# A recommender tower: VectorE turns the samples in 32x32 blocks, and the top layers run in two batches

## The chip, the cores and the metric

The kernel runs on one core of a Trainium2 chip. Its time is the device time of one launch in microseconds (us). Engines are named as in the profile: PE (TensorE matmuls, PEld for the loads of weights), DVE (VectorE), ACT (ScalarE), POOL (GpSimd) and SP (SyncE, which here only issues DMAs). PSUM is the memory of eight banks that matmuls write to, SBUF the memory that all engines share.

## The reference, cut to what matters

For 512 samples, 32 embedding rows of 32 numbers each are gathered from 32 tables. Two layers of a compressed interaction network follow, then three dense layers.

```python
e = stack([tbl_f[ids[:, f]] for f in range(32)], axis=1)      # 512 x 32 fields x 32 dims
x0 = prev = e
for W in (filter_0, filter_1):                                # (32*32 -> 128), (32*128 -> 128)
    z = einsum('bhd,bmd->bhmd', x0, prev).reshape(b, h * m, d)
    prev = relu(einsum('bpd,pn->bnd', z, W[0]))
    outs.append(prev)
z = sum(concatenate(outs, axis=1), axis=-1)                   # 512 x 256
h = concatenate([z, dense_ctx], axis=1)                       # 512 x 272
h = maximum(h @ W_top1 + b_top1, 0)                           # 512 x 512
h = maximum(h @ W_top2 + b_top2, 0)                           # 512 x 256
y = h @ W_top3                                                # 512 x 1
```

Everything is float32. The kernel splits the operands of the large products into a high and a low part and multiplies three pairs of them in the faster fp32r format.

## The kernel before, in words

The 512 samples are four blocks of 128, and the 32 dims are eight groups of 4. A chunk is one block and one group: 128 samples times 4 dims, thus 512 columns. There are 32 chunks. Two chunks make one turn of the loop (UNROLL), and the first and the last turn are written out.

In a chunk PE walks through 32 slots of three matmuls of 512 columns each (line 870): layer 2 of the chunk, into four banks that DVE reads and two that ACT reads. DVE multiplies each 128 columns by a field's number and adds them up (line 762, eight such MACs for four slots); ACT multiplies the other half (line 561) and POOL sums these with accumulating DMAs and adds (lines 358, 365, 372). Between the slots stands the work for the next chunks, each at a slot that a constant gives (lines 51 to 67): DVE multiplies pairs of fields for chunk c + 1 (DVE_PAIR, slots 0, 4, 8 and 12 of chunk c, line 622), ACT and POOL split them (lines 496 and 381), and PE multiplies them with layer 1's filters into cur_bank (PE_PRODUCT, slots 17 to 24, line 808); the product of slot 22 needs DVE's line 626, which stands ahead of DVE's MACs of slot 20.

The pairs need the fields of the samples with the samples along the columns, and shifted copies of them. That is done two chunks ahead, for chunk c + 2 during chunk c. At slot 0 ACT copies the 32 x 4 numbers of each of the 128 samples to turn_in (line 474). At slot 4, after DVE has read the sums out of the same bank (line 641), PE transposes this 128x128 block into cur_bank (line 787). At slot 5 ACT copies it to turned (line 479). SP writes turned to a scratch buffer in DRAM in two DMAs of 512 B rows, the 32 fields and 16 of them once more (line 312), waits for both, and loads it back in six DMAs, once as it is (x4) and five times shifted (shifts, line 320). ACT copies x4 to its PSUM bank at slot 29, and DVE's first pair reads the shifts at slot 0 of chunk c + 1. Every engine runs its own instructions in order; they wait for each other with semaphores alone. A register counts the chunks in the loop.

The start does chunk 0's layer 1 without DRAM: DVE copies the gathered fields in spread order (line 712), PE transposes them (line 839), and DVE multiplies. Chunk 1 already goes through DRAM (the calls with c = 1).

At the end DVE and POOL sum what is left of the last block of 128 samples (lines 769 to 781). PE has by then started top 1: it needs z1 (layer 1's sums), the dense inputs and z2 (layer 2's). z1 and the dense part are multiplied for all 512 samples (lines 901 and 902), z2 for the first 384 (line 905), and then PE waits for the last 128. These are transposed (line 816), copied by ACT (line 592) and multiplied (line 911). Relus on ACT (line 596), top 2 (line 917), relus (line 600), top 3 (line 922), a copy (line 603) and one DMA of the 512 results follow, each over all 512 samples. Float32 matmuls take two instructions each in the profile.

## Time and profile before

| | |
|---|---|
| time, median of 3 runs | 891.64 us (889.85 to 893.33) |
| the profiled execution's own time | 892.28 us |
| its span, first to last instruction | 890.5 us |
| PE busy | 837.7 us, 94% |
| DVE busy | 763.7 us, 86% |
| ACT busy | 727.2 us, 82% |
| POOL busy | 663.0 us, 74% |
| mean granted clock of PE | 0.996 of 2.4 GHz |
| mean traffic of the DMA engines | 140 GB/s |

A busy share is one over the whole span. Matmuls overlap, so a busy PE says less than the distance from one matmul's start to the next one's. In the rows below, what stands in brackets is the idle time of that engine ahead of the instruction and what ended it.

### The profile page before, as it was taken

To read this page: it belongs to the slowest core of one execution; us is meant where nothing else is said; L and a number is where in the kernel's file an instruction comes from. 1 tells how busy PE (TensorE), PEld (TensorE's weight loads), DVE (VectorE), ACT (ScalarE), POOL (GpSimd) and SP (SyncE) were. 2 spreads that over 40 slices of the span, in tenths; PEclk is the share of its full clock that TensorE was granted. 3 is DMA by queue.
4 is the path that set the end of the run, shared out by engine and by line. 5 is a ranking of instruction groups with operands and counts; after the bars stand their busy time and mean duration, and the time that the engine had idled before them with its cause. 6 is when DMAs were issued, how large, how long until landed. Compare 5 with 4: busy or idle time off the path is not lost.

```text
span 890.5 us, 18079 instructions
## 1 busy us (share of the span) xinstructions
PE 837.7 (94%) x3607; PEld 669.2 (75%) x3607; DVE 763.7 (86%) x2394; ACT 727.2 (82%) x2418; POOL 663.0 (74%) x645
## 2 busy tenths in 40 slices
PE   0179999999999999999999999999999999999997
PEld 0158888888888788888888878888888888888873
DVE  4148989999988899999999999999999999999993
ACT  2257889998888899888888889888888989888872
POOL 7776898878787888878888888866666676666651
PEclk9999999999999999999999999999999999999999
DMA  7035776667667666667567656676577656665450
GB/s 195 13 91 123 173 167 147 147 128 156 152 149 165 161 155 148 132 146 160 145 158 173 157 139 136 140 166 144 146 169 169 150 144 128 138 159 145 79 95 0
DMA packets 59773, 124.40 MB, mean 140 GB/s; under 512 B 9377, under 2 KB 18145, under 8 KB 59746
## 3 DMA queue, kind: packets, MB, share of 16 engines
q0 software_dynamic: 22240, 68.17, 40.8%
q1 hardware_dynamic: 37506, 55.96, 19.7%
q14 instruction: 21, 0.17, 0.1%
q8 instruction: 6, 0.10, 0.0%
HBM read 54.99 MB, written 3.05 MB: 65 GB/s over the span
## 4 chain that ended last, share of the span: by engine, by line
PE 79%; POOL 9%; issue 4%; DVE 4%; DMA 2%; ACT 0%; SPq 0%; DVEq 0%; POOLq 0%; ACTq 0%
PE bank L870 67%; PE bank L808 10%; POOL rows L346 4%; DVE acc L762 2%; POOL pair_low L381 2%; POOL rows_next L396 1%; POOL parts L358 1%; PE bank L917 1%; POOL w_sb L365 1%; DMA parts<-parts 1%; PE bank L876 1%; DMA shifts<-x_scratch 1%; PE bank L787 0%; POOL half L365 0%; DVE acc L772 0%
## 5 line engine op out<-in xcount | busy, mean ns | idle before, releaser
L561 ACT ACTIVATE parts<-bank,x 128x128 f32<-128x128 f32 x2048 | 590.2, 380 | 99.0 <-PE bank L870 88.5
L762 DVE SCALAR_TENSOR_TENSOR acc<-bank,x,acc 128x128 f32<-128x128 f32 x1792 | 484.7, 341 | 45.0 <-PE bank L870 44.9
L870 PE MATMUL bank<-w_high,cur_high 128*128 128x512 f32 x1024 | 403.8, 394 | 3.2 <-DVE acc L762 2.4
L870 PE MATMUL bank<-w_low,cur_high 128*128 128x512 f32 x1024 | 399.9, 391 | 0.0
L870 PE MATMUL bank<-w_high,cur_low 128*128 128x512 f32 x992 | 388.6, 392 | 0.0
L870 PEld LDWEIGHTS bank<-w_high,cur_high 128*128 128x128 f32 x1024 | 192.6, 188 | 46.0 <-DVE acc L762 3.4
L870 PEld LDWEIGHTS bank<-w_low,cur_high 128*128 128x128 f32 x1024 | 192.7, 188 | 40.4
L870 PEld LDWEIGHTS bank<-w_high,cur_low 128*128 128x128 f32 x992 | 186.5, 188 | 40.6
L381 POOL TENSOR_TENSOR pair_low<-pair,pair_high 128x512 fp32r<-128x512 f32 x124 | 158.7, 1300 | 27.9 <-ACT pair_high L496 25.5
L365 POOL TENSOR_TENSOR half<-parts 128x512 f32<-128x512 f32 x64 | 82.8, 1294 | 93.0 <-DMA parts<-parts 92.9
L396 POOL DMA_INDIRECT rows_next<-table_dram,ids_next x96 | 98.0, 1021 | 30.6 <-issue 30.3
L358 POOL DMA_DIRECT2D parts<-parts x126 | 114.5, 1070 | 4.4 <-issue 4.3
L622 DVE TENSOR_TENSOR pair<-bank,shifts 128x512 f32<-128x512 f32 x124 | 84.2, 679 | 4.9 <-DMA shifts<-x_scratch 4.9
L365 POOL TENSOR_TENSOR w_sb<-parts 128x512 f32<-128x512 f32 x62 | 80.1, 1313 | 3.1 <-DMA parts<-parts 3.0
L496 ACT CAST pair_high<-pair 128x512 fp32r<-128x512 f32 x124 | 79.8, 644 | 2.0 <-DVE pair L622 2.0
L762 DVE SCALAR_TENSOR_TENSOR acc<-bank,x,parts 128x128 f32<-128x128 f32 x128 | 41.7, 346 | 16.0 <-PE bank L870 12.6
L808 PE MATMUL bank<-pair_high,w_low 128*128 128x512 f32 x124 | 49.2, 397 | 0.0
L808 PE MATMUL bank<-pair_high,w_high 128*128 128x512 f32 x124 | 48.9, 394 | 0.2
L808 PE MATMUL bank<-pair_low,w_high 128*128 128x512 f32 x124 | 49.0, 395 | 0.0
L822 PE MATMUL bank<-w_high 128*128 128x512 f32 x16 | 5.7, 531 | 40.9 <-DMA rows<-table_dram,ids_sb 40.9
L372 POOL TENSOR_TENSOR w_sb<-half 128x512 f32<-128x512 f32 x32 | 41.4, 1294 | 3.5
L346 POOL DMA_INDIRECT rows<-table_dram,ids_sb x32 | 34.4, 1074 | 12.1 <-issue 9.4
(92 smaller groups left out, 551.9 us busy)
## 6 DMA issues: line engine op xcount, KB each, us to landing
parts<-parts POOLq DMA_DIRECT2D x126, 512.0 KB, 6.1
shifts<-x_scratch SPq DMA_DIRECT2D x155, 256.0 KB, 3.9
x<-x_scratch SPq DMA_DIRECT2D x31, 256.0 KB, 2.9
x_scratch<-turned SPq DMA_DIRECT2D x31, 64.0 KB, 4.0
rows_next<-table_dram,ids_next POOLq DMA_INDIRECT x96
wt<-w_top_dram SPq DMA_DIRECT2D x2, 512.0 KB, 8.9
x_scratch<-turned SPq DMA_DIRECT2D x31, 32.0 KB, 3.9
rows<-table_dram,ids_sb POOLq DMA_INDIRECT x32, 2.4
```

The costliest lines, as they stand in the source:

```text
L346: nc.gpsimd.indirect_dma_start(out=rows[:, 0, f, :], out_offset=None, in_=tables[f], in_offset=bass.IndirectOffsetOnAxis(ids_sb[:, 0, f:f ...
L358: nc.gpsimd.dma_start(parts[q][ab][:, 0:width], parts[q][ab][:, width:2 * width], accum_op=ALU.add).then_inc(added[ab], 16)
L365: nc.gpsimd.tensor_tensor(half[t // 2 % 2][:, t % 2, :], src[:, 0:512], src[:, 512:1024], ALU.add).then_inc(tree, 1)
L372: nc.gpsimd.tensor_tensor(left[:, t % DC:t % DC + 2, :, :].rearrange("p t l n -> p t (l n)"), half[t // 2 % 2][:, :, 0:256], half[t // 2 % ...
L381: nc.gpsimd.tensor_tensor(pair_low[step - 1][:], pair[step - 1], pair_high[step][:].bitcast(FP32), ALU.subtract).then_inc(pair_low_done, 1)
L396: nc.gpsimd.indirect_dma_start(out=rows_next[:, f, :], out_offset=None, in_=tables[f], in_offset=bass.IndirectOffsetOnAxis(ids_next[:, f:f ...
L496: nc.scalar.copy(pair_high[step][:], pair[step - 1]).then_inc(pair_high_done, 1)
L561: ins = nc.scalar.activation(parts[q][ab][:, at:at + N2], act_bank[ab][:, i * N2:(i + 1) * N2], ACT.Copy, scale=x0[u][:, h, 2 * q + ab:2 * ...
L622: nc.vector.tensor_tensor(dst[:], fields, shifted, ALU.mult).then_inc(paired, 1)
L762: nc.vector.scalar_tensor_tensor(out=dst, in0=dve_bank[e % 2 * 2 + ab][:, i * N2:(i + 1) * N2], scalar=x0[u][:, h, 2 * q + ab:2 * q + ab + ...
L808: ins = nc.tensor.matmul(cur_bank[:], filters, products, start=step == order[0] and i == 0, stop=step == order[-1] and i == len(terms) - 1)
L870: return nc.tensor.matmul(dst[:], cur_half[u][:, cols], w1_half[:, fields], **flags)
```

## The change

The transposition for the way through DRAM moves from PE to DVE, whose transposition turns each 32x32 block by itself. turn_in and turned now hold the 16 repeated fields too (192 columns), which ACT copies at slot 0 with a second, smaller copy. DVE transposes at slot 8, ahead of that slot's pair. Which block goes where is left to the DMAs: SP writes four of them, one for each 32 partitions, in runs of 32 numbers. PE's transposition, ACT's copy out of PSUM and their semaphore go.

The top layers run for samples 0 to 383 and for the last 128 in turn, each with PSUM banks of its own. PE multiplies everything of the 384 that is known, the known part of the last 128, and half of top 2 of the 384 ahead of the transposition of the last z2; then the other half, and the rest of the last 128 behind it. ACT's relus and copies are split alike. SP waits for two copies of results and sends one DMA as before.

```diff
-ACT_TURN, PE_TURN, ACT_TURNED = 0, 4, 5
+ACT_TURN, DVE_TURN = 0, 8
+QUAD = 32
...
-        turn_in = sb("turn_in", [P, DC * F])
-        turned = sb("turned", [P, P])
+        turn_in = sb("turn_in", [P, DC * (F + SHIFTS)])
+        turned = sb("turned", [P, DC * (F + SHIFTS)])
...
-        a1_bank, a2_bank, y_bank = [bank[4], bank[5], bank[7], dve_bank[0]], dve_bank[1:3], dve_bank[3]
+        a1_bank, last_a1_bank = [x4_bank] + act_bank + [dve_bank[0]], dve_bank[1:4] + [cur_bank]
+        a2_bank, last_a2_bank = [x4_bank, act_bank[0]], [dve_bank[0], act_bank[0]]
+        last_z2_bank = act_bank[1]
+        y_bank, last_y_bank = x4_bank, act_bank[1]
...
-        WRITES, LOADS = 2, STEPS
+        WRITES, LOADS = P // QUAD, STEPS
...
                 sp.wait_ge(turned_ready, c)
                 to = x0_dram[u]
-                for first_field, fields in ((0, F), (F, SHIFTS)):
-                    if first_field > 0:
-                        wait(sp, paired, (c - 1) * STEPS)
-                    sp.dma_start(to[first_field:first_field + fields, :].rearrange("f (d b) -> (f d) b", d=DC),
-                                 turned[0:fields * DC, :]).then_inc(written, 16)
+                for b in range(0, P, QUAD):
+                    dst = bass.AP(to.tensor, to.offset + b, [[P, QUAD], [QUAD * P, (F + SHIFTS) * DC // QUAD], [1, QUAD]])
+                    sp.dma_start(dst, turned[b:b + QUAD, :].rearrange("i (k j) -> i k j", j=QUAD)).then_inc(written, 16)
                 sp.wait_ge(written, c * (WRITES * 16))
...
         def act_turn(act, c):
-            nc.scalar.copy(turn_in[:].rearrange("p (f d) -> p f d", d=DC), rows_of(c)).then_inc(turn_ready, 1)
-
-        def act_turned(act, c):
-            act.wait_ge(transposed, c)
-            wait(act, written, (c - 1) * (WRITES * 16))
-            nc.scalar.copy(turned[:], turn_bank[:, 0:P]).then_inc(turned_ready, 1)
+            fields = turn_in[:].rearrange("p (f d) -> p f d", d=DC)
+            nc.scalar.copy(fields[:, 0:F, :], rows_of(c)).then_inc(turn_ready, 1)
+            nc.scalar.copy(fields[:, F:, :], rows_of(c)[:, 0:SHIFTS, :]).then_inc(turn_ready, 1)
...
+        def dve_turn(dve, c):
+
+            dve.wait_ge(turn_ready, 2 * c)
+            wait(dve, written, (c - 1) * (WRITES * 16))
+            nc.vector.transpose(turned[:], turn_in[:]).then_inc(turned_ready, 1)
...
             first_copy(F - LAST_TABLES, F - LAST_TABLES, F)
+            dve_turn(dve, 1)
             dve.wait_ge(first_fields_ready, 3)
...
+                            if slot == DVE_TURN and not last:
+                                dve_turn(dve, c + 2)
                             if slot == DVE_SUM:
...
-        def pe_turn(pe, c):
-            pe.wait_ge(turn_ready, c)
-            wait(pe, summed, c - 1)
-            nc.tensor.transpose(turn_bank[:, 0:P], turn_in[:], ident[:]).then_inc(transposed, 1)
...
             if step == order[0]:
                 wait(pe, summed, c)
-                if turn:
-                    pe.wait_ge(turned_ready, c + 1)
...
             for i in range(H1 // P):
-                n = slice(i * P, (i + 1) * P)
                 if a1_bank[i] is x4_bank:
                     pe.wait_ge(folded, CHUNKS - 1)
+                elif a1_bank[i] is act_bank[0]:
+                    pe.wait_ge(act_prod, PAIRS * (2 * EACH))
                 if i == H1 // P - 1:
                     pe.wait_ge(mac, PAIRS * (2 * MACS) - 2 * HG)
-                nc.tensor.matmul(a1_bank[i][:], wt1[:, 0, n], z1[:], start=True, stop=False)
-                nc.tensor.matmul(a1_bank[i][:], wt1_dense[:, n], dense_sb[:], start=False, stop=False)
+                top1_known(a1_bank[i][:, three], i, three)
             pe.wait_ge(z2_ready, 1)
             for i in range(H1 // P):
-                nc.tensor.matmul(a1_bank[i][:, 0:B - P], wt1[:, 1, i * P:(i + 1) * P], z2[:, 0:B - P], start=False,
-                                 stop=False)
-            pe_z2(pe, BLOCKS - 1, BLOCKS)
+                nc.tensor.matmul(a1_bank[i][:, three], wt1[:, 1, i * P:(i + 1) * P], z2[:, three], start=False,
+                                 stop=True).then_inc(top_product, 1)
+            pe.wait_ge(mac, PAIRS * (2 * MACS))
+            for i in range(H1 // P):
+                top1_known(last_a1_bank[i][:, 0:P], i, last)
+            top2(a2_bank[0][:, three], 0, three, 0)
+            pe.wait_ge(z2_step, 4)
+            nc.tensor.transpose(last_z2_bank[:, 0:P], z2_rows[:, BLOCKS - 1, :], ident[:]).then_inc(z2_turned, 1)
+            top2(a2_bank[1][:, three], 1, three, 0)
             pe.wait_ge(z2_ready, 2)
             for i in range(H1 // P):
-                n = slice(i * P, (i + 1) * P)
-                nc.tensor.matmul(a1_bank[i][:, B - P:], wt1[:, 1, n], z2[:, B - P:], start=False,
+                nc.tensor.matmul(last_a1_bank[i][:, 0:P], wt1[:, 1, i * P:(i + 1) * P], z2[:, last], start=False,
                                  stop=True).then_inc(top_product, 1)
...
+            top3(y_bank[0:1, three], three, H1 // P)
+            top2(last_a2_bank[0][:, 0:P], 0, last, THREE_PRODUCTS)
+            top2(last_a2_bank[1][:, 0:P], 1, last, THREE_PRODUCTS)
+            top3(last_y_bank[0:1, 0:P], last, THREE_PRODUCTS + H1 // P)
```

top1_known multiplies z1 and the dense part, top2 and top3 run the four and the two products of a group of outputs, each behind the relus that it needs; three and last are the columns 0 to 383 and 384 to 511. ACT takes, in order: the four relus of the 384, the copy of the last z2, the two relus of top 2 of the 384, the four relus of the last 128, the copy of the 384 results, the two relus of the last 128, and their copy.

## Rows read from the trace of the kernel before

**Rows 1.** The page's chain that ended last, shares of the span by engine.

```profile
PE 79%; POOL 9%; issue 4%; DVE 4%; DMA 2%; ACT 0%; SPq 0%; DVEq 0%; POOLq 0%; ACTq 0%
```

**Rows 2.** PE: timelines around two transpositions (start, us, what), a chain piece, a wait.

```profile
392.36 0.39 PE L870 MATMUL bank<-w_high,cur_low 128*128 128x512 f32 x1
392.93 0.39 PE L870 MATMUL bank<-w_low,cur_high 128*128 128x512 f32 x1
...
417.45 0.39 PE L870 MATMUL bank<-w_high,cur_low 128*128 128x512 f32 x1
418.22 0.40 PE L870 MATMUL bank<-w_low,cur_high 128*128 128x512 f32 x1
...
843.48 4.55 PE bank L870 x20
...
PEld bank L787 <- issue: 4.2, 13, 0.4
```

**Rows 3.** Timelines of DVE and PE over a chunk; one group by lines.

```profile
406.31 0.69 DVE L626 TENSOR_TENSOR pair_hl<-bank,pair_hl 64x512 fp32r<-64x512 f32 x1
407.14 0.41 PE L808 MATMUL bank<-pair_hl,w_half_hl 128*128 128x512 f32 x1
...
422.88 0.68 DVE L622 TENSOR_TENSOR pair<-bank,shifts 128x512 f32<-128x512 f32 x1
423.47 2.15 DVE L762 SCALAR_TENSOR_TENSOR acc<-bank,x,acc 128x128 f32<-128x128 f32 x8
429.27 0.74 DVE L762 SCALAR_TENSOR_TENSOR acc<-bank,x,parts 128x128 f32<-128x128 f32 x2 [0.39 <-PE bank L870]
...
L762 DVE SCALAR_TENSOR_TENSOR acc<-bank,x,parts 128x128 f32<-128x128 f32 x128 | 41.7, 346 | 16.0 <-PE bank L870 12.6 <-ACT parts L561 2.1
```

**Rows 4.** Groups by line: a DVE operation on 384 words.

```profile
L651 DVE TENSOR_TENSOR rows_next<-w_sb 128x384 f32<-128x384 f32 x1 | 0.6, 558 | 0.0
```

**Rows 5.** DMA queues and landings (page), and timelines of SP and DVE.

```profile
q0 software_dynamic: 22240, 68.17, 40.8%
q1 hardware_dynamic: 37506, 55.96, 19.7%
...
shifts<-x_scratch SPq DMA_DIRECT2D x155, 256.0 KB, 3.9
...
420.90 1.65 SPq L312 DMA_DIRECT2D x_scratch<-turned  x2
425.95 3.13 SPq L320 DMA_DIRECT2D shifts<-x_scratch  x5
...
442.58 0.68 DVE L622 TENSOR_TENSOR pair<-bank,shifts 128x512 f32<-128x512 f32 x1
```

**Rows 6.** Timeline of the start, and a window (PE, PEld, DVE, ACT, POOL busy; PEclk, DMA).

```profile
49.05 1.09 PE L839 MATMUL bank<-ident,parts 128*128 128x128 f32 x8 [2.41 <-DVE parts L712]
51.56 0.92 SPq L312 DMA_DIRECT2D x_scratch<-turned  x2
62.63 0.69 DVE L622 TENSOR_TENSOR pair<-bank,shifts 128x512 f32<-128x512 f32 x1 [4.94 <-DMA shifts<-x_scratch]
65.45 0.79 PE L870 MATMUL bank<-w_high,cur_high 128*128 128x512 f32 x1 [2.41 <-DVE acc L762]
...
65.40:68.70 3.30, 3.25 (x8) 2.58 (x9) 3.26 (x10) 1.62 (x7) 2.90 (x4) 0.50 0.19 45
```

**Rows 7.** PE's timeline of the end, and a window of it (columns as above).

```profile
865.84 1.10 PE L901 MATMUL bank<-x,wt 128*128 128x512 f32 x2 [0.65 <-ACT parts L561]
870.27 2.74 PE L905 MATMUL bank<-pair,wt 128*128 128x384 f32 x8
875.61 0.33 PE L816 MATMUL bank<-ident,rows_next 128*128 128x128 f32 x1 [2.59 <-DVE rows_next L780]
876.29 1.16 PE L911 MATMUL bank<-pair,wt 128*128 128x128 f32 x8 [0.35 <-ACT pair L592]
886.38 1.88 PE L922 MATMUL bank<-w_sb,wt 128*1 128x512 f32 x4
...
877.60:881.30 3.70, 3.68 (x5) 1.64 (x6) 0.00 (x0) 1.70 (x3) 0.00 (x0) 0.54 0.00 0
```

More of the change, by code:

```diff
@@ L29 @@
 BLOCKS = B // P
+THREE = B - P
 DC = 4
@@ L206, in dlrm_tower @@
         turn_ready = sem("turn_ready")
-        transposed = sem("transposed")
         turned_ready = sem("turned_ready")
@@ L578, in body @@
                                     act_x4(act, c + 2, u)
-                                if slot == ACT_TURNED and not last:
-                                    act_turned(act, c + 2)
                                 if slot == ACT_Z2 and last and u == UNROLL - 1:
                                     act.wait_ge(z2_turned, 1)
-                                    nc.scalar.copy(z2[:, 0:B - P], turn_bank[:, 0:B - P]).then_inc(z2_ready, 1)
+                                    nc.scalar.copy(z2[:, 0:B - P], z2_bank[:, 0:B - P]).then_inc(z2_ready, 1)
             body_loop(act, body)
@@ L881, in body @@
                                 if slot in PE_PRODUCT and not (last and u == UNROLL - 1):
-                                    pe_product(pe, c + 1, PE_PRODUCT[slot], turn=not last)
-                                if slot == PE_TURN and not last:
-                                    pe_turn(pe, c + 2)
+                                    pe_product(pe, c + 1, PE_PRODUCT[slot])
                                 if slot == PE_Z2 and last and u == UNROLL - 1:
@@ L893, in _, with top1_known, top2 @@
             pe.wait_ge(z1_step, 2)
-            pe.wait_ge(act_prod, PAIRS * (2 * EACH))
+            three, last = slice(0, THREE), slice(THREE, B)
+            def top1_known(dst, i, columns):
+                n = slice(i * P, (i + 1) * P)
+                nc.tensor.matmul(dst, wt1[:, 0, n], z1[:, columns], start=True, stop=False)
+                nc.tensor.matmul(dst, wt1_dense[:, n], dense_sb[:, columns], start=False, stop=False)
+            def top2(dst, m, columns, relus_before):
+                for i in range(H1 // P):
+                    pe.wait_ge(top_relu, relus_before + i + 1)
+                    ins = nc.tensor.matmul(dst, wt2[:, i, m * P:(m + 1) * P], a1[:, i, columns], start=i == 0,
+                                           stop=i == H1 // P - 1)
+                ins.then_inc(top_product, 1)
@@ L895, in _, with top3 @@
+            def top3(dst, columns, relus_before):
+                for i in range(H2 // P):
+                    pe.wait_ge(top_relu, relus_before + i + 1)
+                    ins = nc.tensor.matmul(dst, wt3[:, i:i + 1], a2[:, i, columns], start=i == 0,
+                                           stop=i == H2 // P - 1)
+                ins.then_inc(top_product, 1)
             for i in range(H1 // P):
-                n = slice(i * P, (i + 1) * P)
                 if a1_bank[i] is x4_bank:
                     pe.wait_ge(folded, CHUNKS - 1)
+                elif a1_bank[i] is act_bank[0]:
+                    pe.wait_ge(act_prod, PAIRS * (2 * EACH))
@@ L920, in _ @@
-            for k in range(H2 // P):
-                pe.wait_ge(top_relu, H1 // P + k + 1)
-                ins = nc.tensor.matmul(y_bank[0:1, :], wt3[:, k:k + 1], a2[:, k, :], start=k == 0,
-                                       stop=k == H2 // P - 1)
-            ins.then_inc(top_product, 1)
+            top3(y_bank[0:1, three], three, H1 // P)
+            top2(last_a2_bank[0][:, 0:P], 0, last, THREE_PRODUCTS)
+            top2(last_a2_bank[1][:, 0:P], 1, last, THREE_PRODUCTS)
+            top3(last_y_bank[0:1, 0:P], last, THREE_PRODUCTS + H1 // P)
```

45 lines of the change are left out of this document (24 added, 21 removed).

## The prediction

> **What bounds the kernel now.** I read the page's chain that ended last first: PE has 79% of the span [rows 1]. Nearly all of that is the chunk loop, so the next question is how tight PE runs there and what else runs as tight. The timeline of PE shows matmuls that start every 0.2275 us (4.55 us for 20 [rows 2]); a chunk has 109 of them (32 slots of 3, and 13 for the next chunk's products), 24.8 us. So PE sets the pace, and time is won in the loop only where a matmul start is late. One such place is the transposition, at slot 4.
>
> The second view is VectorE's timeline over one chunk, because DVE is busy 86% of the span and PE's banks come free by its MACs. DVE runs without a pause from the MACs of slot 20 of one chunk to those of slot 12 of the next; only ahead of slot 16 does it wait for PE, 0.39 us in the chunk shown, and 12.6 us in all such waits, 0.41 us in each of 31 chunks [rows 3]. Ahead of slot 20 it waits another 1.4 us, but that is no spare time: DVE's low half of pair 16 (L626) ends at 407.00, PE's product that needs it starts at 407.14, and the MACs of slot 20 need the matmuls right behind that product [rows 3]. So PE and DVE form a ring through L626, the product of slot 22, slot 23 and the MACs of slot 20, and DVE's spare time per turn of the ring is the 0.41 us, and some 0.08 us of the 0.14 between L626 and the product: 0.49 us beside a PE that still has its transposition.
>
> The third view is the timeline of the end. PE is idle from 873.0 (870.27 + 2.74) to 875.61, when DVE's last sums reach it, and only then runs the last quarter of top 1, all of top 2 and top 3 in a row until 888.26; the granted clock was 0.54 from 877.6 to 881.3 (1.2 GHz for most of it), behind that idle time [rows 7].
>
> **The loop: what PE gives back.** In one chunk of two kinds the transposition costs PE 392.93 - 392.36 = 0.57 us for two matmul steps that take 0.455 without it, so 0.115; in the other kind 418.22 - 417.45 = 0.77, so 0.315, since it waits there for DVE's sum (L641) too; 13 of the 30 in the loop are of that kind [rows 2]. Together 13 x 0.315 + 17 x 0.115 = 6.1 us, 0.20 us a chunk. That is all that leaving it out can give: 6.1 us, if nothing takes its place. The wait for the sum goes too; pe_product keeps its own wait for summed, but 13 slots later.
>
> **The loop: what DVE takes on.** One transposition of 128x192 words a chunk, 30 times, ahead of the pair of slot 8, thus in the part without a pause. No row shows such an operation. A 128x512 pair takes 0.68 us and the next operation starts 0.59 after it (422.88 to 423.47 [rows 3]), so 0.09 of a duration is overlapped; a 128x384 add takes 0.56 [rows 4], so a word costs about 0.95 ns and 192 words some 0.37 us, which is 0.29 of DVE's time. Ends: nothing at all (0, if it ran inside gaps), and 0.59, what a 512-word operation takes. I take 0.30, next to the 384-word row. With PE 0.20 faster the ring leaves DVE 0.49 - 0.20 = 0.29 us: just used up. Two parties with no slack do not meet exactly in both kinds of chunk, so I take 0.04 a chunk off: the period falls by 0.16 us, 30 x 0.16 = 4.8 us. At 0.59 it would rise by 0.59 - 0.49 = 0.10, 3 us lost.
>
> The Trainium skill, "VectorE: DVE Perf Modes", section "The three transpose paths", has 390 ns on TensorE and 311 ns on VectorE for 128x128 in bf16, and says that VectorE turns 32x32 blocks only. By 311 x 1.5 = 0.47 us (an estimate from that page; no run here shows it), 0.38 of DVE's time, the loop would give 2.1 us (30 x 0.07) instead of 4.8; and its 390 ns is not what leaving out the PE transposition is worth here, since rows 2 show 0.12 to 0.32.
>
> **ACT, SP and the DMA queue.** ACT loses the PSUM copy of slot 5 and gets a 128x64 copy at slot 0, both about 0.3 us; it waits for PE again within the same chunk, so nothing. SP issues four writes in place of two, at 0.4 to 0.5 us each (0.92 for two [rows 6]), and its wait for paired goes, which DVE's order implies. The transposed rows are ready at about 423.3 in place of 420.9; the five shift loads were issued until 429.08 and land in 3.9; the next chunk's first pair reads them at 442.58 [rows 5]. So 442.6 - 433.0 = 9.6 us spare, less 2.4 for the later start and 0.9 for two more issues: 6.3 us are left for slower writes. The writes turn from 192 packets of 512 B into 768 of 128 B, 48 on each of 16 engines in place of 12. SP's queue spent 19.7% x 16 x 890.5 / 37506 = 75 ns on a packet [rows 5]: 36 more are 2.7 us, inside the 6.3. Costed at nothing. Later loads meet the accumulating DMAs longer; POOL, which waits for those, has its results used some chunk later.
>
> **The start.** The transposition of chunk 1 now stands on DVE ahead of the copies that PE's first transposes wait for (49.05), so that chain starts about 0.9 us later (the wait for ACT's two copies, and 0.37). But PE stood still for 2.41 us at 65.45 anyway, because DVE waited 4.94 us for chunk 1's shifts; the clock was 0.50 behind it [rows 6]. What counts is when the shifts land. The writes can be issued from about 49.6 in place of 51.56, the last of four at 51.0 in place of 52.0, so 1 us earlier; 36 packets more on each engine take from nothing to 2.7 us. Between 1 us won and 1.7 lost I take 0; should the stall shrink enough to keep the clock, 1.6 us more come back (eight matmuls at 0.43 for 0.23).
>
> **The end.** Work on 384 columns costs three quarters of that on 512. The order of PE after the loop, from rows 7:
> - known products of the 384: PE now starts with the bank that is free at once (x4_bank), so up to 0.65 us earlier (its wait for ACT at 865.84); four took (870.27 - 865.84) = 4.43, now 3.3: 865.2 to 868.5; z2's products 2.74: 871.3;
> - known products of the last 128: four at a quarter of 4.43 and some overhead, 1.5: 872.8;
> - top 2, first half of the outputs, 384 columns, 8 instructions as those of L905: 2.74: 875.55. ACT's relus run beside it. All that fills the idle time.
> - DVE's last sums come at 875.6 as before: transposition 0.33, 875.95; second half of top 2, 2.74: 878.7, which hides ACT's copy of z2; last quarter of top 1, 1.16: 879.85; top 3 of the 384, three quarters of 1.88: 881.25;
> - top 2 of the last 128, twice 1.16: 883.55; its last relu, 0.35 (as the gap ahead of 876.29): 883.9; top 3's last two instructions 0.3: 884.2 in place of 888.26.
>
> That is 4.1 us, and the copy of 128 results in place of 512 perhaps 0.1: 4.2. Of it, about 1.8 is the clock, which I expect to stay at 2.4 GHz since PE is no longer idle ahead of it. The lower end is 2.2 (the clock at half for as long as before), the upper 5.
>
> **Sum.** 4.8 + 0 + 4.2 = 9.0 us. The profiled execution took 892.28 (span 890.5 and 1.8 around it), so 883.3; it lies 0.64 above the median of 891.64, so I forecast 882.6. Best ends: 6.1 + 2.6 + 5 = 13.7, 878; worst of the plain terms: loop -3, end 2.2, start -1.7: 894.
>
> **Rivals.**
> 1. *DVE becomes the bound.* The transposition takes 0.45 to 0.59 of its time (blocks filled and drained, an operation that overlaps less). For: a pause of 0.41 us a chunk is all that DVE has. Against: it is shorter than any of the 512-word operations. Loop from 0.0 to -3, end 4.2: 887.4 to 890.5.
> 2. *The end keeps its half clock, or ACT's chain of small relus stretches it.* For: the clock fell once there, and the last stretch has short matmuls. Against: no PE idle time over 0.4 us in the new order. End 2.2 in place of 4.2: 884.6.
> 3. *Slower: the writes come too late.* Place: SP's wait for the four writes, and behind it six loads; it decides once the writes take over 6.3 us longer. At what a packet cost on POOL's queue (40.8% x 16 x 890.5 / 22240 = 261 ns [rows 5]) 36 more packets are 9.4 us: 3.1 us a chunk, 93 us over 30, about 975. Against: SP's own queue shows 75 ns. In the Trainium skill, "DMA: Bandwidth & Descriptors", the table "Specifications" asks for 512 B or more for line rate and has a read-modify-write below that; this rule speaks against the change, 512 to 128 B, and no run here shows what such writes to DRAM cost.
> 4. *The split does nothing*, since top 2's second half stands ahead of the last quarter of top 1: the end gives 1, 885.8. Against: that half hides ACT's copy and would have to run anyway.
>
> **How the numbers follow.** Forecast 0.57, rival 1 0.17, rival 2 0.16, rival 3 0.06, rival 4 0.04. Half a per cent, about what a measurement tells from no change, is 4.5 us: faster is below 887.2, slower above 896.1. Forecast, rivals 2 and 4 fall under faster (0.77) and the lucky end of rival 1 adds 0.03; the rest of rival 1 and a hundredth of rival 3 give same, 0.15; the rest of rival 3 slower, 0.05. The range runs from the best ends, 878, to the far end of rival 1, 890, and leaves out rival 3 and what overruns the ends.
>
> **What would show it.** No L787 on PE, and 0.2275 us between all starts around slot 4; the transposition at about 0.37 us on DVE with a following start 0.3 later; DVE's wait ahead of slot 16 gone, a chunk period of 25.0 us in place of 25.16; no wait of DVE or ACT for shifts or x4 beyond the first chunk; PE without idle time over 0.5 us behind the loop, clock 1.0, and its end 4 us earlier in relation to the last MAC. Wrong: a chunk period at or above 25.16, waits of L626's product that grow, shifts that land after the next chunk begins, or a clock of 0.5 in the end.

## The result, and the profile after

The changed kernel takes 886.12 us (median of 6 runs, 882.99 to 888.07) against 890.50 us for the kernel before on the same chip (6 runs); the ratio is 0.9947, with a 95% interval from 0.9932 to 0.9962. The time lies inside the range and the sign was right, but 4.4 us came where 9.0 were forecast. The profiled execution took 882.99 us, span 881.2; it is the fastest of the six, so a second profile of the same kernel (changed_again, below, 886.55 us) stands beside it wherever the two differ.

The first thing to read is where the time of a span lies. The cuts are the starts of the first matmul with cur_low in chunk 1 and in chunk 31 (line 876 before, 885 after):

| us | before | after | changed_again |
|---|---|---|---|
| start and chunk 0 | 86.61 | 84.92 | 84.74 |
| chunks 1 to 30 | 756.48 | 753.72 | 756.15 |
| chunk 31 and the end | 47.41 | 42.56 | 43.81 |
| span | 890.5 | 881.2 | 884.7 |

So in the execution nearer to the median the loop won little, and of the 4.85 us that chunk 31 and the end won in the other, 3.6 were left; where those 1.25 us lie is shown behind the end's profile.

The chain that ended last still belongs to PE (it answers to [rows 1]):

```profile
PE 80%; POOL 9%; issue 5%; DVE 3%; DMA 2%; ACT 0%; POOLq 0%; DVEq 0%; ACTq 0%
```

PE around slot 4 of the same chunk as in [rows 2] (start, duration, what): the starts are 0.23 us apart, and no transposition stands between them.

```profile
388.86 0.39 PE L879 MATMUL bank<-w_low,cur_high 128*128 128x512 f32 x1
389.09 0.39 PE L879 MATMUL bank<-w_high,cur_low 128*128 128x512 f32 x1
389.32 0.39 PE L879 MATMUL bank<-w_high,cur_high 128*128 128x512 f32 x1
```

DVE, against [rows 3, 4]: the transposition with the operation behind it, the MACs of slot 16 and the low half of pair 16 in the next chunk's timeline; then the transposition's line (duration in ns, least/median/greatest), and the group of MACs that waited at slot 16.

```profile
394.23 0.36 DVE L637 STREAM_TRANSPOSE turned<-turn_in 128x192 f32<-128x192 f32 x1
394.52 0.65 DVE L631 TENSOR_TENSOR pair<-bank,shifts 128x512 f32<-128x512 f32 x1
...
426.55 0.74 DVE L780 SCALAR_TENSOR_TENSOR acc<-bank,x,parts 128x128 f32<-128x128 f32 x2
428.87 0.70 DVE L641 TENSOR_TENSOR pair_hl<-bank,pair_hl 64x512 fp32r<-64x512 f32 x1
...
L637 DVE STREAM_TRANSPOSE turned<-turn_in x31: 358/366/379, 49.6 to 796.4; 128x192 f32<-128x192 f32 x31
...
L780 DVE SCALAR_TENSOR_TENSOR acc<-bank,x,parts 128x128 f32<-128x128 f32 x128 | 41.8, 346 | 6.5 <-ACT parts L560 3.3 <-PE bank L879 1.2
```

The next operation starts 0.29 us after the transposition, and the pause ahead of slot 16 is gone: 6.5 us in that group in place of 16.0, of it 1.2 for PE in place of 12.6. A chunk that nothing disturbs now takes 25.04 us in place of 25.17 (medians of the odd and of the even chunks, averaged).

SP's queue and the landings of the page, and SP's issues for chunk 16's way through DRAM, answer to [rows 5]:

```profile
q1 hardware_dynamic: 56354, 55.96, 21.0%
...
parts<-parts POOLq DMA_DIRECT2D x126, 512.0 KB, 6.7
shifts<-x_scratch SPq DMA_DIRECT2D x155, 256.0 KB, 3.9
...
420.73 1.81 SPq L316 DMA_DIRECT2D x_scratch<-turned  x4
424.41 3.11 SPq L323 DMA_DIRECT2D shifts<-x_scratch  x5
```

The shifts land as fast as before. The accumulating DMAs (parts<-parts) land later, after 6.7 us where the page of before has 6.1, and POOL waits longer for them. Its largest waits in the kernel before (us in total, times, longest):

```profile
POOL half L365 <- DMA parts<-parts: 92.9, 58, 3.9
POOL mark L355 <- DVE parts L762: 27.3, 25, 2.0
```

The same two waits in the changed kernel:

```profile
POOL half L368 <- DMA parts<-parts: 119.9, 60, 5.9
POOL mark L358 <- DVE parts L780: 1.7, 6, 0.4
```

The 27.3 us for which POOL waited at the mark, the instruction ahead of the next accumulating DMA, were its spare time. After, that wait is 1.7 us. Where the spare time runs out shows in chunk 13, which took 25.11 us before and 25.85 after. Timelines of SP, POOL and PE there, in the kernel before:

```profile
374.94 0.53 SPq L320 DMA_DIRECT2D x<-x_scratch  x1
...
380.20 1.83 POOL L358 DMA_DIRECT2D parts<-parts  x2
385.58 1.29 POOL L365 TENSOR_TENSOR half<-parts 128x512 f32<-128x512 f32 x1 [3.55 <-DMA parts<-parts]
...
390.72 1.04 POOL L422 COPY rows<-rows_next 128x1024 f32 x1
403.43 2.55 POOL L381 TENSOR_TENSOR pair_low<-pair,pair_high 128x512 fp32r<-128x512 f32 x2
...
405.51 0.40 PE L870 MATMUL bank<-w_high,cur_low 128*128 128x512 f32 x1
405.75 0.39 PE L808 MATMUL bank<-pair_high,w_high 128*128 128x512 f32 x1
```

The same instructions of chunk 13 in the changed kernel:

```profile
373.42 0.53 SPq L323 DMA_DIRECT2D x<-x_scratch  x1
...
377.04 1.84 POOL L361 DMA_DIRECT2D parts<-parts  x2
383.75 1.29 POOL L368 TENSOR_TENSOR half<-parts 128x512 f32<-128x512 f32 x1 [4.87 <-DMA parts<-parts]
...
388.87 1.04 POOL L425 COPY rows<-rows_next 128x1024 f32 x1
401.57 2.53 POOL L384 TENSOR_TENSOR pair_low<-pair,pair_high 128x512 fp32r<-128x512 f32 x2
...
402.09 0.40 PE L879 MATMUL bank<-w_high,cur_low 128*128 128x512 f32 x1
402.90 0.50 PE L819 MATMUL bank<-pair_high,w_high 128*128 128x512 f32 x1 [0.42 <-POOL pair_low L384]
```

Read from top to bottom: the loads start 5.26 us ahead of the accumulating DMA before, and 3.62 after. The DMA lands in 5.38 and in 6.71 us. Behind it on POOL stand the sums, the copy of the next block's rows (only in chunks 5, 13 and 21, where a block of samples is changed), a copy of row numbers, the next accumulating DMA, two gathers of rows (from 392.78 to 395.17 after; they and the copy of row numbers are missing in chunk 21), and then the splits of the pairs. Before, the pair that the product needs is split at 404.7 (half of the two from 403.43), 1.05 us ahead of PE's product at 405.75; after, at 402.84, and the product's start is 0.81 us behind the matmul ahead of it where 0.23 is the pace. Chunk 21 is in time in every profile, though it has the copy too: without the gathers its split is ready 13.9 us behind the chunk's first matmul with cur_low in place of 16.3.

The start, against [rows 6]: the first pair, and the window where PE stood still before (busy time and instructions of PE, PEld, DVE, ACT, POOL; PEclk, DMA share, GB/s).

```profile
60.68 0.69 DVE L631 TENSOR_TENSOR pair<-bank,shifts 128x512 f32<-128x512 f32 x1 [0.28 <-DMA shifts<-x_scratch]
...
65.40:68.70 3.30, 3.30 (x16) 2.72 (x15) 3.30 (x13) 3.24 (x12) 2.90 (x4) 1.00 0.13 21
```

The wait for shifts is 0.28 in place of 4.94 us, and PE runs 16 matmuls in a window that had 8, at a granted clock of 1.00 in place of 0.50. But PE's first transposes now run at 0.50 (50.3 to 52.5), behind an idle time of 2.48 us; before, they ran at 1.00 behind 2.41. This is not the change's own: top_only and end_warm below, which keep the old start, have the half clock there too, and turn_only, which has the new one, has not.

The end, PE's timeline and a window over all of it, against [rows 7]:

```profile
860.62 0.81 PE L905 MATMUL bank<-x,wt 128*128 128x384 f32 x2
...
863.91 2.74 PE L932 MATMUL bank<-pair,wt 128*128 128x384 f32 x8
...
867.78 2.79 PE L911 MATMUL bank<-w_sb,wt 128*128 128x384 f32 x8
871.27 0.33 PE L939 MATMUL bank<-ident,rows_next 128*128 128x128 f32 x1 [0.70 <-DVE rows_next L798]
871.44 2.75 PE L911 MATMUL bank<-w_sb,wt 128*128 128x384 f32 x8
874.02 1.05 PE L943 MATMUL bank<-pair,wt 128*128 128x128 f32 x8
875.00 1.45 PE L918 MATMUL bank<-w_sb,wt 128*1 128x384 f32 x4
876.38 2.05 PE L911 MATMUL bank<-w_sb,wt 128*128 128x128 f32 x16
878.37 0.91 PE L918 MATMUL bank<-w_sb,wt 128*1 128x128 f32 x4
...
860.00:881.20 21.20, 18.42 (x85) 11.70 (x83) 11.00 (x17) 7.68 (x20) 5.14 (x6) 1.00 0.00 1
```

From the transposition of the last z2 to PE's last end it is 8.01 us (871.27 to 879.28); before it was 12.65 (875.61 to 888.26). The clock stays at 1.00, though PE still waits 0.70 us for the last z2.

This stretch takes 8.00 us in changed_again as well. What is longer there lies in chunk 31, where DVE's first sum for z1 and POOL's sum of parts run beside each other. The two in the profile of after, then in changed_again:

```profile
845.61 2.43 POOL L368 TENSOR_TENSOR w_sb<-parts 128x512 f32<-128x512 f32 x1 [2.90 <-DMA parts<-parts]
845.67 1.22 DVE L755 TENSOR_TENSOR w_sb<-sum 128x1024 f32<-128x1024 f32 x1
...
847.81 1.29 POOL L368 TENSOR_TENSOR w_sb<-parts 128x512 f32<-128x512 f32 x1 [2.90 <-DMA parts<-parts]
847.93 2.26 DVE L755 TENSOR_TENSOR w_sb<-sum 128x1024 f32<-128x1024 f32 x1
```

One of the two takes 1.0 to 1.1 us longer than the other time. Where POOL's record starts 0.06 us or less ahead of DVE's, POOL's is the long one; where it starts 0.09 us or more ahead, DVE's is, DVE's next MACs come later, and PE's last matmul of the chunk is 1.3 us late (0.8 in light_halves). This holds in all 14 profiles: the kernels with PE's transposition are all of the first kind, those with DVE's all of the second, except the profile of after. Why POOL comes some 0.05 us sooner there was not tested.

### The profile page after: what moved, and what is told of

It is laid out like the page before. It is cut to its first block, busy times and chain, and to the rows that moved or that the text cites. A ratio compares the mean times of both kernels' runs of the same rounds, so it can differ in the third digit from the quotient of the medians.

```text
span 881.2 us, 18094 instructions
## 1 busy us (share of the span) xinstructions
PE 832.6 (94%) x3608; PEld 669.4 (76%) x3608; DVE 771.7 (88%) x2425; ACT 724.7 (82%) x2425; POOL 662.0 (75%) x645
## 4 chain that ended last, share of the span: by engine, by line
PE 80%; POOL 9%; issue 5%; DVE 3%; DMA 2%; ACT 0%; POOLq 0%; DVEq 0%; ACTq 0%
PE bank L879 68%; PE bank L819 10%; POOL rows L349 4%; DVE acc L780 2%; POOL pair_low L384 2%; DMA parts<-parts 1%; POOL w_sb L368 1%; POOL rows_next L399 1%; PE bank L885 1%; POOL parts L361 1%; PE bank L911 1%; PE bank L850 1%; DVE acc L790 0%; POOL half L368 0%; DMA rows<-table_dram,ids_sb 0%
## 5 line engine op out<-in xcount | busy, mean ns | idle before, releaser
L879 PEld LDWEIGHTS bank<-w_high,cur_high 128*128 128x128 f32 x1024 | 192.3, 188 | 48.2 <-DVE acc L780 6.4
L375 POOL TENSOR_TENSOR w_sb<-half 128x512 f32<-128x512 f32 x32 | 41.4, 1294 | 3.6
```

The costliest lines, as they stand in the source:

```text
L375: nc.gpsimd.tensor_tensor(left[:, t % DC:t % DC + 2, :, :].rearrange("p t l n -> p t (l n)"), half[t // 2 % 2][:, :, 0:256], half[t // 2 % ...
L879: return nc.tensor.matmul(dst[:], cur_half[u][:, cols], w1_half[:, fields], **flags)
```

## The experiments

All are timed beside the kernel before. "Late" chunks are those over 0.3 us above the undisturbed period; 8, 9 and 18 are late in every kernel, by 1.8 us in sum in the profile of before, where it is always PE's product with pair_high and w_high that starts late (0.44 to 0.50 us behind the matmul ahead of it).

| kernel | median us (runs) | before | ratio [95%] | undisturbed period | late, us | chunk 31 and end |
|---|---|---|---|---|---|---|
| changed_again | 885.83 (6) | 890.41 | 0.9939 [0.9922, 0.9955] | 25.04 | 4.9 | 43.8 |
| turn_only | 890.29 (12) | 890.41 | 0.9996 [0.9984, 1.0009] | 25.03 | 5.1 | 48.3 |
| top_only | 885.53 (5) | 890.41 | 0.9935 [0.9922, 0.9949] | 25.18 | 2.2 | 42.5 |
| turn_slot4 | 887.55 (7) | 890.41 | 0.9968 [0.9949, 0.9988] | 25.10 | 5.0 | 43.8 |
| small_runs | 893.37 (9) | 890.79 | 1.0030 [1.0017, 1.0043] | 25.19 | 2.4 | 47.2 |
| late_before | 890.71 (12) | 890.79 | 1.0002 [0.9991, 1.0013] | 25.19 | 1.7 | 48.2 |
| top_turn6 | 883.36 (5) | 890.79 | 0.9911 [0.9898, 0.9924] | 25.07 | 3.0 | 42.5 |
| turn_twice | 890.02 (12) | 890.79 | 0.9989 [0.9980, 0.9999] | 25.19 | 4.5 | 43.8 |
| light_halves | 885.71 (5) | 891.10 | 0.9940 [0.9926, 0.9953] | 25.03 | 4.7 | 43.3 |
| light_before | 890.10 (11) | 891.10 | 0.9991 [0.9982, 1.0000] | 25.18 | 2.3 | 48.3 |
| end_warm | 889.32 (11) | 891.10 | 0.9981 [0.9972, 0.9990] | 25.18 | 3.2 | 45.8 |
| long_runs | 885.31 (5) | 890.65 | 0.9949 [0.9935, 0.9962] | 25.05 | 4.6 | 43.9 |

**The two parts alone.** First the changed kernel again, then each half of the change on the kernel before.

> The changed kernel as it is, for its spread. The six executions known so far run from 882.99 to 888.07 us, with the profiled one at the lowest; the forecast's sum holds in that one (9.3 us against 9.0), so the 3.5 us between it and the median are what is to be explained. Theory A (POOL falls behind: the shift loads now start 2.7 us later and meet the accumulating DMAs that POOL waits for, and in the profiled execution POOL's waits for those are already 119.9 us against 92.9): the median is 885 to 887 again, and this profile, if it is of a slower execution, shows more stretches in which the product of pairs waits for pair_low (3 in the first profile), each with a chunk period of 25.7 us or more; first and last chunk as in the first profile. Theory B (the start or the clock): the chunk periods are as in the first profile (mean 25.13 us over 29 chunks), and the difference lies ahead of chunk 1 or behind chunk 31.

turn_only has DVE's transposition and the four writes with the old top layers; top_only has the new top layers with PE's transposition:

```diff
 turn_only
-ACT_TURN, PE_TURN, ACT_TURNED = 0, 4, 5
+ACT_TURN, DVE_TURN = 0, 8
...
 top_only
-        a1_bank, a2_bank, y_bank = [bank[4], bank[5], bank[7], dve_bank[0]], dve_bank[1:3], dve_bank[3]
...
+        a2_bank, last_a2_bank = [x4_bank, act_bank[0]], [dve_bank[0], act_bank[0]]
...
```

> Only the transposition on DVE and its writes; the top layers as before the change. Theory A: the loop's gain of 2.8 us and the start's 2 are mostly lost in most executions, so 888 to 890 us, with the same spread of some 5 us. Theory B: 885 to 887 where the start goes well, and a spread that comes from the start. Forecast of the prediction for this part alone: 4.8 us won.

> Only the top layers in two batches; the transposition on PE as before. Both theories: the end gains 4.5 to 4.9 us as in the first profile of the changed kernel (47.4 us from the last chunk's start to the end against 42.6), so 885.6 to 886.2 us, and the spread is that of the kernel before (under 1.5 us in five of six executions). If the end's gain depends on how PE leaves the loop, it is under 3 us here.

In changed_again theory A holds for the loop: the median is 885.83 and PE waits four times for pair_low, 2.2 us in all. But 1.25 us of the difference between the two profiles lie in chunk 31, which neither theory named. top_only alone wins 4.9 us and turn_only 0.1, so the whole gain that can be measured is the end's. In turn_only the undisturbed period does fall by 0.13 us, 30 x 0.134 = 4.0 us, but chunks 5 and 13 are late by 0.8 and 1.9 us, and 8, 9 and 18 a little later than before: 5.1 - 1.8 = 3.3 us are given back. The rest went in chunk 31, which is 1.3 us longer there by DVE's long sum. From the transposition of the last z2 on, that profile is 0.4 us shorter (12.26 us against 12.65), so that chunk 31 and the end together have 48.3 us against 47.4; kernels with the old end take 12.3 to 13.5 us for that last stretch.

**When the way through DRAM starts.** The changed kernel with the transposition at slot 4:

```diff
-ACT_TURN, DVE_TURN = 0, 8
+ACT_TURN, DVE_TURN = 0, 4
```

> The changed kernel with DVE's transposition at slot 4 in place of 8: the writes and loads start 2.7 us earlier, about where they were before the change. Theory A: POOL's waits for the accumulating DMAs fall back towards 93 us, pair_low is late less often, and the median falls to 882 to 883.5 with a smaller spread. Theory B: no change against the changed kernel (885 to 887). A third possibility: PE waits at slot 13 for the MACs of slot 4, which now end 0.3 us later with 0.2 to spare; then the period grows by about 0.1 us and the median is 887 or more.

The median, 887.55 us, is that of the third possibility, though the period grew by 0.06 us only. The late chunks stay (5.0 us), because the loads did not start earlier: at slot 4 the four writes took 3.41 us to issue and SP's loads came 6.45 us behind the first of them (3.67 in the changed kernel, both in chunk 12).

Two experiments put one half each of what the change does to the way through DRAM into the kernel before: runs of 128 B in four writes at the old slot, and the old two writes four slots later.

```diff
 small_runs
-        WRITES, LOADS = 2, STEPS
+        WRITES, LOADS = 4, STEPS
...
+                    for half in range(2):
+                        n, at = fields * DC, half * F
+                        dst = bass.AP(to.tensor, to.offset + first_field * COLS + at, [[P, n], [2 * F, 2], [1, F]])
...
 late_before
-ACT_TURN, PE_TURN, ACT_TURNED = 0, 4, 5
+ACT_TURN, PE_TURN, ACT_TURNED = 0, 4, 9
```

> The kernel before, with PE's transposition, but the same bytes written in four DMAs of 128 B runs in place of two of 512 B runs (768 packets a chunk in place of 192). Theory A1 (the short runs hold up the accumulating DMAs that POOL waits for): POOL's waits for those rise from 93 to 110 us or more, its wait for DVE ahead of the next pair falls from 27 to under 8, parts lands in 6.5 us or more, more products wait for pair_low, and the time is 891 to 893. Theory A2 (the later start of writes and loads does it): POOL's waits stay under 97 us and the time is within 1 us of the kernel before.

> The kernel before, but ACT copies PE's transposed block out at slot 9 in place of 5, so that writes and loads start 1.5 to 2.7 us later; everything else, the 512 B runs too, as before. A1: POOL's waits for the accumulating DMAs stay under 97 us and the time is within 1 us of the kernel before. A2: they rise to 110 us or more and the time is 891 to 893. If both this and the short runs raise them by some 10 us, it is both.

Each takes part of POOL's spare time without a measurable stall in the loop: POOL waits 106.2 and 109.0 us for its DMAs (92.9 before), which land in 6.6 us, and its spare time at the mark falls to 14.5 and 10.9 us. By these waits it is both, as the expectation has it; A2's time for late_before, 891 to 893, did not come. small_runs loses 2.6 us, and its one profile puts most of them at the start, not in the loop: 86.90 us against 84.4 in late_before, both at a granted clock of 1.00, with chunk 1's loads 4.35 us behind its first write where the kernel before has 2.23. (The profile of before has 86.61 there for another reason: its clock fell to 0.50 behind DVE's wait for shifts.) Neither alone gives back in the loop what turn_only gives back.

**Is it that POOL has too much to do?** The changed kernel, and the kernel before, with POOL's last addition on half its columns:

```diff
-                nc.gpsimd.tensor_tensor(left[:, t % DC:t % DC + 2, :, :].rearrange("p t l n -> p t (l n)"),
-                                        half[t // 2 % 2][:, :, 0:256], half[t // 2 % 2][:, :, 256:512], ALU.add).then_inc(tree, 1)
+                nc.gpsimd.tensor_tensor(left[:, t % DC:t % DC + 1, :, :].rearrange("p t l n -> p t (l n)"),
+                                        half[t // 2 % 2][:, 0:1, 0:256], half[t // 2 % 2][:, 0:1, 256:512], ALU.add).then_inc(tree, 1)
```

> The changed kernel, but POOL's last add of each pair of tiles (sum_halves) covers half of its columns, so half of layer 2's sums on POOL are left out; POOL saves some 0.57 us twice a chunk and nothing else changes. Theory POOL (the loop's gain is lost because POOL has no slack left beside the slower accumulating DMAs): POOL's wait for DVE ahead of the next pair comes back to 20 us or more, the late chunks (5, 8, 9, 13, 18) shrink to under 2 us of excess in all, and the median falls from 885.8 to 882 to 883.5. Theory DVE and PE alone (the ring is the bound and POOL's waits are only its symptom): no change, 885 to 886.5.

> The same edit on the kernel before (half of POOL's last add left out). It has 27 us of slack on POOL already and three late chunks of 1.75 us in all. Theory POOL: 0 to 1.7 us faster, 889 to 890.7, so that the changed kernel with this edit leads it by 6.5 to 7.5 us in place of 4.6. If the lead stays 4.6, POOL is not where the loop's gain went.

My theory there was POOL's work, and its forecasts fell: the lead over light_before is 4.4 us, the late chunks stayed (4.7 us), and POOL spent the time that it was given in the same wait (us, times, longest, in light_halves):

```profile
POOL half L368 <- DMA parts<-parts: 140.7, 62, 6.5
```

In chunk 13 POOL issues the accumulating DMA 0.56 us earlier than in changed_again (10.07 us ahead of the chunk's first matmul with cur_low in place of 9.51), yet the first sum starts 2.04 us ahead of that matmul in place of 2.16: the landing did not follow the issue. The late chunks also have a second cause there. PE's wait for pair_low is only 0.06 us in that chunk (0.91 in changed_again), but PE then waits 0.52 us for DVE's low half of pair 16, since ACT waited 1.33 us for POOL's sum of parts and DVE 1.13 us for ACT. A late landing thus reaches PE in two ways, and the edit shortens the second by half as much as the first.

**Is it the short runs?** The changed kernel, with each write storing one run of 768 B for each partition:

```diff
-                    dst = bass.AP(to.tensor, to.offset + b, [[P, QUAD], [QUAD * P, (F + SHIFTS) * DC // QUAD], [1, QUAD]])
+                    dst = bass.AP(to.tensor, to.offset + b * (F + SHIFTS) * DC, [[(F + SHIFTS) * DC, QUAD], [1, (F + SHIFTS) * DC]])
```

> The changed kernel, but each of the four writes stores its 32 partitions in runs of 192 numbers (768 B) one behind another, as many bytes at the same slot; the scratch buffer then holds the numbers in another order, so the fields are mixed (the operands have other values, the work is the same). Theory A, the short runs of 128 B give the gain back: POOL's waits for its DMAs fall from 120 to some 108 us as in late_before, the median landing of its accumulating DMAs from 6.7 to 6.5 or less, the rows copies of chunks 5 and 13 are within 1.6 us of their chunk's first matmul, PE is not late in these two chunks, and the time falls by 1.5 to 3 us below the changed kernel's 886: 883 to 884.5. Theory B, it is the later writes and loads with the shorter period, whatever the runs: landing 6.6 or more, chunks 5 and 13 as late as before (0.6 to 1.9 us), 885.5 to 886.5. If only SP's issue of four writes counts, nothing moves either, and the start's wait for shifts stays near 0.3 us.

Theory B holds in the time, in the landing (6.7 us) and in chunk 5, which is late by 1.3 us; chunk 13 is in time. With a third fewer packets on SP's queue POOL waits as long. SP's queue on the page of long_runs, and POOL's wait:

```profile
q1 hardware_dynamic: 36514, 55.96, 20.0%
...
POOL half L368 <- DMA parts<-parts: 119.0, 61, 5.6
```

What goes with the lateness of chunks 5 and 13 is when the loads start. This table has chunks 5 and 13 of several kernels, from the timelines of SP, POOL and PE; the first two columns are measured from the chunk's first matmul with cur_low, and the last is the chunk's time above the undisturbed period.

| kernel, chunks 5 / 13 | loads start | rows copied | accumulating DMA issued to its second sum | late |
|---|---|---|---|---|
| before | -14.9 / -14.9 | 0.3 / 0.9 | 7.4 / 7.9 | 0 / 0 |
| late_before | -14.1 / -14.1 | 1.6 / 1.6 | 8.2 / 8.6 | 0 / 0 |
| small_runs | -13.8 / -14.5 | 1.8 / 0.9 | 7.6 / 7.9 | 0.2 / 0 |
| long_runs | -13.0 / -14.0 | 2.8 / 1.4 | 8.4 / 8.0 | 1.3 / 0 |
| after | -13.8 / -13.2 | 1.5 / 2.3 | 7.9 / 9.2 | 0 / 0.8 |
| changed_again | -13.1 / -13.1 | 2.4 / 2.9 | 8.0 / 9.8 | 0.9 / 1.4 |
| turn_only | -13.2 / -13.2 | 2.3 / 3.4 | 9.0 / 10.3 | 0.8 / 1.9 |
| turn_slot4 | -12.6 / -13.1 | 2.4 / 2.1 | 8.1 / 8.3 | 0.9 / 0.6 |
| light_halves | -13.3 / -13.2 | 2.7 / 2.5 | 10.7 / 10.5 | 1.2 / 1.0 |

In these two chunks, wherever the loads start at -13.8 or earlier the chunk is in time to 0.2 us; wherever they start at -13.3 or later, POOL's copy comes at 2.1 or later and the chunk is late. Even one kernel's two chunks part by this (after, long_runs). Without the copy and the gathers such a start does no harm: chunks 6, 10 and 14 of after have their loads at -13.0, -13.1 and -12.8 and are in time. With the copy alone, chunk 21 of turn_slot4 has its rows copied at 2.2 and is in time too.

That later transfers lengthen the accumulating DMA is what late_before shows: it moves only them and ACT's copy ahead of them, the loads by 0.8 us, and has 0.8 and 0.7 us more in the fourth column (in one profile; before, top_only and end_warm, whose loads start at -14.9, have 7.3 to 7.9). That this goes by way of the DMA engines is the reading that fits the trace's packets. From the DMA's issue to the second sum in chunk 13, SP's queue had packets under way for 1.57 us of the 16 engines' time before and for 2.86 after, 1.29 more, and the second sum came 1.30 us later (7.92 and 9.22); POOL's queue had 5.49 and 5.30 us. In the first 5 us the engines were busy throughout in both (DMA share 1.03 and 1.00). No run took the loads off these engines to prove it. In chunk 5 of changed_again only 0.6 of the 2.1 us come this way; the other 1.4 are the DMA's issue, at -8.3 in place of -9.7, since POOL, with its spare time at the mark gone, had not caught up from the late landing of half a chunk earlier.

**Is DVE's time used up?** The changed kernel with a second transposition, of 128 words, that nobody reads:

```diff
+            nc.vector.transpose(spare_turned[:], turn_in[:, 0:P])
```

> The changed kernel with a second transposition on DVE in each chunk, of 128x128 words into a buffer that nobody reads (some 0.22 us of DVE's time). Ring theory (DVE has no spare time left after the change): the period of undisturbed chunks rises from 25.03 to 25.2 or 25.25 us, 5 to 6.5 us in 30 chunks; POOL gets slack back, so up to 2.5 us of its late chunks go, and the time is 888.5 to 891. Theory that POOL alone sets the pace of the changed loop: under 1 us more, 885 to 887.

The spare transposition among the groups by line of turn_twice (busy us, mean ns of one, idle time before):

```profile
L638 DVE STREAM_TRANSPOSE spare_turned<-turn_in 128x128 f32<-128x128 f32 x31 | 9.2, 298 | 0.5 <-ACT turn_in L480 0.5
```

The spare transposition delays DVE's next operation by 0.225 us. The undisturbed period rises by 0.15 us, 30 x 0.146 = 4.4, and the time by 4 us: in the changed kernel DVE has next to no time left in the ring (0.08 us by these numbers), as the prediction had it. The late chunks did not shrink (4.5 us).

**What of the end is the clock?** The kernel before, with ten spare matmuls in PE's idle time ahead of the last z2:

```diff
+            pe.wait_ge(mac, PAIRS * (2 * MACS))
+            keep_busy(10, dve_bank[3])
```

> The kernel before with ten matmuls of 512 columns that nobody reads in PE's idle time of 2.6 us, ahead of the transposition of the last z2; nothing else changes. It parts the end's 4.8 us into the clock and the rest. Forecast by its steps: the clock stays at 2.4 GHz behind it and 1.8 us come back, 888.6 to 889; if the clock has no part in it, 890.4; if the dummy matmuls delay the transposition, up to 0.3 us are lost of that.

PE's timeline of the end in end_warm, and a window behind it (columns as above):

```profile
875.24 0.33 PE L816 MATMUL bank<-ident,rows_next 128*128 128x128 f32 x1 [0.45 <-DVE rows_next L780]
...
877.00:881.00 4.00, 3.83 (x10) 1.82 (x10) 0.00 (x0) 1.94 (x5) 0.00 (x0) 1.00 0.00 0
```

PE's idle time ahead of the transposition falls from 2.59 to 0.45 us, the clock behind it is 1.00 in place of 0.54, and 1.8 us are won (891.10 to 889.32). That is the clock's part of the end's 4.9 (with the interval of the table, 0.9 to 2.5); by subtraction, the order of the work is the other 3.1.

**A version without the loss.** top_only with PE's transposition moved to slot 6 and ACT's copy to slot 8:

```diff
-ACT_TURN, PE_TURN, ACT_TURNED = 0, 4, 5
+ACT_TURN, PE_TURN, ACT_TURNED = 0, 6, 8
```

> The top layers in two batches, PE's transposition kept, but at slot 6 in place of 4 (ACT's copy at slot 8), where DVE has long read its sum out of the same bank. 13 of 30 transpositions cost PE 0.32 us in place of 0.12 since they wait for that sum; here all should cost 0.12. Theory A1: 2.5 us less than the top layers alone, 883 to 884, as the short runs are not there. A2: the later start of the loads costs POOL its slack and the time is 885 to 887. If PE's loop is not the bound between the late products, no change: 885.5.

PE around the transposition in the chunk of [rows 2]:

```profile
393.49 0.39 PE L887 MATMUL bank<-w_high,cur_low 128*128 128x512 f32 x1
393.72 0.27 PE L804 MATMUL bank<-ident,turn_in 128*128 128x128 f32 x1
393.74 0.48 PE L887 MATMUL bank<-w_high,cur_high 128*128 128x512 f32 x1
394.06 0.40 PE L887 MATMUL bank<-w_low,cur_high 128*128 128x512 f32 x1
```

The transposition no longer waits for DVE's sum and costs 394.06 - 393.49 - 0.455 = 0.115 us in every chunk. The undisturbed period falls by 0.11 us, the loads of chunks 5 and 13 start at -14.6 and -14.7, both are in time, and the time is 2.2 us below top_only's: 883.36 us, the best of all here, with ratio 0.9911 where the change has 0.9939 and 0.9947.

## Why the prediction was half right

- **That the time lies inside the range** is in part luck. The range reached to 890 for a longer transposition, which did not come; the loss that did come stands in no term of the sum. By the runs the sum is 4.0 (loop) - 3.1 (late chunks) - 1.3 (chunk 31) + 4.9 (end) = 4.5 us, where 4.4 were measured.
- **What PE gives back** was read rightly: 0.23 us between all starts around slot 4. top_turn6, which takes away the 13 waits for DVE's sum alone, confirms these: 2.2 us won, where 13 x 0.2 = 2.6.
- **DVE's transposition** was sized rightly, 0.366 us (0.37 forecast) and 0.29 to the next start (0.30). In the Trainium skill, "VectorE: DVE Perf Modes", section "The three transpose paths", VectorE's figure is 311 ns for 128x128 in bf16; turn_twice shows 298 for 128x128 in f32, so the page's figure fits to 13 ns, for another type. What failed was the estimate from it, 0.47: the time does not grow in proportion to the words, since 64 words more took 68 ns.
- **The ring** held: the pause ahead of slot 16 is used up and the undisturbed period fell by 0.13 us (0.16 forecast), 4.0 us of 4.8; turn_twice confirms that DVE has next to nothing left then.
- **The failed step is "Costed at nothing" for ACT, SP and the DMA queue**, with its sentence that POOL's results are used "some chunk later". The 6.3 us spare were rightly counted for the shifts: beyond the first chunk DVE never waits for them. But they were counted for that reader alone. POOL's own spare time, 27.3 us at the mark in the profile before, was never read, and POOL's next work behind the wait is the split of pairs that PE needs within the same chunk, with 1.05 us to spare in chunk 13. In chunks 5 and 13 the loads start 1.1 to 1.8 us later in relation to the chunk, the accumulating DMA lands later, and behind it the copy and two gathers leave POOL no time, so the chunks are late. The loop gave back about 3 us in changed_again and turn_only and 1 us in the fastest execution, of the 4.0 won. The 1.3 us of chunk 31 come on top in every profile with DVE's transposition but that of after (0.8 in light_halves); the prediction has no term for them.
- **The start**, taken as 0, came out near it. Of the 1.7 us between the two profiles, most is not the change: late_before and top_only, which keep the old start, have 84.4 and 84.9 us there, the changed kernel 84.7 and 84.9.
- **The end**, 4.2 forecast, gave 4.85 between the two profiles and 4.9 in top_only, of it 1.8 the clock as forecast. PE was to have no idle time over 0.5 us there; it had 0.70, and the clock stayed. The batch of 128 costs less than I took: twice 1.03 us for top 2 (2.05) in place of twice 1.16.
- **The rivals.** Rival 1 did not come: the transposition was not longer. Its time, 887.4 to 890.5, starts 1.3 us above the median all the same, for another reason. Rival 2 did not: the clock stays. Rival 3 had the right place, SP's wait for the writes, but the wrong price and the wrong victim: the added 19,840 packets that long_runs takes away cost (21.0% x 881.2 - 20.0% x 883.4) x 16 / 19,840 = 7 ns each, far from 75 or 261. In the Trainium skill, "DMA: Bandwidth & Descriptors", the table "Specifications" asks for 512 B for line rate; long_runs (768 B) and the change (128 B) differ by no measurable time. Rival 4 did not come: the end gave 4.9, not 1.

Open: what makes the product of chunks 8, 9 and 18 late in every kernel, why POOL comes sooner in chunk 31, and what makes one execution of the changed kernel 5 us slower than another. Of the 3.5 us between its two profiled spans 2.4 are the loop's and 1.3 chunk 31's.

## What to carry to other kernels

Before a transfer is moved, list every engine that waits for DMAs in that stretch, not just the reader of the transfer, and read each one's spare time as what it waits for *other* things. A gain per turn of a loop can be given back in the few turns that carry extra work, so compare the times of single turns, not only their mean. In a tail, put known work into the wait for the last result: here it filled the idle time, and the clock stayed at 1.00.

## What was not expected of the hardware

Four writes issued at slot 4 took 3.41 us of SP's time and their loads followed 6.45 us after the first; the same writes at slot 8 took 1.76 and 3.67 (chunk 12). Relieved of 0.56 us of each addition (738 in place of 1294 ns), POOL did not get ahead: its wait for the accumulating DMAs grew from 120 to 141 us. And in chunk 31 a lead of 0.06 or 0.09 us decides whether POOL's sum or DVE's takes 1 us longer.
